# New instruction orders on four engines, the logits' copy on ScalarE and later pad writes in a one-core routing and expert kernel

## The reference, cut to what matters

```
x = x + L(layernorm(x))          # L: linear recurrent attention over T = 2048, B = 2, D = 256, 4 heads
    v = x @ W_write.T;  scores = (x_t . x_{s-1}) * decay;  reads = scores @ v + state @ x
    out + (alpha * reads) @ W_read.T
x = x + ffn(layernorm(x))        # ffn: 8 experts, each token through its best two
    logits = x @ gate_w.T; probs = softmax(logits); top 2
    h = gelu(x @ w1[e] + b1[e]); y = h @ w2[e] + b2[e]; sum over the two, times probs
```

## Time and profile before

| | us |
|---|---|
| median of 3 runs (lowest, highest) | 580.96 (578.54, 581.52) |
| the profiled execution | 579.32 |
| its span in the trace | 577.5 |
| PE / DVE / ACT / POOL busy | 532.7 / 457.7 / 332.8 / 243.4 |
| recurrent part and its overlap with the first tiles | 0 to about 205 |
| expert part | from 178, PE the bound after about 220 |

### The profile page before, as it was taken

The page is one execution under the profiler, slowest core; times in us unless marked ns, Lnnn a source line. Parts: engine busy times, 40 slices in busy tenths (PEclk is TensorE's granted clock), DMA queues, the critical chain, the costliest instruction groups (busy, mean ns, idle before and its releaser), DMA issues.

```text
span 577.5 us, 17639 instructions
## 1 busy us (share of the span) xinstructions
PE 532.7 (92%) x5246; PEld 417.3 (72%) x5246; DVE 457.7 (79%) x1408; ACT 332.8 (58%) x841; POOL 243.4 (42%) x275
## 2 busy tenths in 40 slices
PE   7788899897988977999999999999999999999991
PEld 7667777786777655777777777777777777777770
DVE  5889999998877789777787877787777887877761
ACT  5889888898735743454545444544454545444540
POOL 2425778887655632332233222333332333222333
PEclk8999999999899999999999999999999999999996
DMA  5667776867234442544443344444444443445432
GB/s 160 208 211 227 252 257 218 264 200 256 75 104 113 124 75 39 82 65 70 69 65 61 61 68 75 78 75 75 69 72 68 66 65 56 68 68 75 76 48 27
DMA packets 85097, 63.34 MB, mean 110 GB/s; under 512 B 54224, under 2 KB 77392, under 8 KB 85008
## 3 DMA queue, kind: packets, MB, share of 16 engines
q1 hardware_dynamic: 71328, 43.94, 30.0%
q0 software_dynamic: 13392, 18.27, 17.2%
q10 hardware_dynamic: 288, 0.00, 0.0%
HBM read 37.56 MB, written 24.62 MB: 108 GB/s over the span
## 4 chain that ended last, share of the span: by engine, by line
PE 60%; DVE 13%; POOL 9%; issue 8%; DMA 5%; ACT 2%; SPq 1%; another core or an unknown queue 0%; DVEq 0%; ACTq 0%; POOLq 0%
PE psum L1514 27%; PE psum L1529 18%; PE psum L1531 9%; POOL sent_rows L497 4%; DMA out<-arena,tile_in 2%; POOL tiny L487 2%; DVE arena L911 1%; DVE weights L775 1%; DMA arena<-sent_rows 1%; POOL tiny L484 1%; PE psum L1424 1%; PE psum L1334 1%; PE psum L1417 1%; PE psum L1345 1%; POOL out L528 1%
## 5 line engine op out<-in xcount | busy, mean ns | idle before, releaser
L1514 PE MATMUL psum<-arena,weights 128*128 128x256 f16 (+1 forms) x2208 | 278.7, 248 | 3.5 <-ACT arena L733 2.1
L1514 PEld LDWEIGHTS psum<-arena,weights 128*128 x2208 | 186.9, 98 | 81.9 <-issue 6.5
L733 ACT ACTIVATE arena<-psum,b_cur 128x256 f32<-128x256 f32 (+1 forms) x368 | 131.7, 424 | 157.7 <-PE psum L1514 119.9
L528 POOL DMA_INDIRECT out<-arena,tile_in x71 | 115.4, 1625 | 251.2 <-DVE arena L1157 147.0
L1529 PE MATMUL psum<-weights,arena 128*128 x568 | 214.7, 379 | 4.2 <-DVE arena L1144 3.9
L1531 PE MATMUL psum<-weights,arena 128*128 x568 | 154.8, 273 | 0.0
L1144 DVE TENSOR_TENSOR arena<-arena 128x512 f16<-128x512 f32 x142 | 99.6, 701 | 4.9
L497 POOL DMA_INDIRECT sent_rows<-arena,tiny x64 | 65.3, 1020 | 26.0 <-issue 18.3
L1142 DVE CAST arena<-arena 128x512 f16<-128x512 f32 x142 | 61.5, 433 | 7.3 <-ACT arena L733 6.6
L1529 PEld LDWEIGHTS psum<-weights,arena 128*128 128x128 f16 x568 | 55.5, 98 | 11.2 <-issue 5.3
L1531 PEld LDWEIGHTS psum<-weights,arena 128*128 128x128 f16 x568 | 55.6, 98 | 4.6 <-issue 0.2
(11 more groups left out here) (172 smaller groups left out, 643.4 us busy)
## 6 DMA issues: line engine op xcount, KB each, us to landing
weights<-in_experts SPq DMA_DIRECT2D x32, 512.0 KB, 4.5
arena<-sent_rows SPq DMA_DIRECT2D x100, 64.0 KB
arena<-in_b SPq DMA_DIRECT2D x46, 128.0 KB
arena<-in_x SPq DMA_DIRECT2D x16, 256.0 KB, 3.2
out<-arena SPq DMA_DIRECT2D x16, 256.0 KB
arena<-sent_rows SPq DMA_DIRECT2D x84, 32.0 KB
sent_rows<-pad SPq DMA_DIRECT2D x7, 265.0 KB
tile_in<-sent_rows SPq DMA_DIRECT2D x71, 4.5 KB, 3.0
```

Source lines behind the costliest of these rows:

```text
L528: pool.indirect_dma_start(out=out, out_offset=bass.IndirectOffsetOnAxis(ap=at_u, axis=0), in_=yout[:, u % 4], in_offset=None, compute_op=A ...
L733: last = a.activation(act[:, g % 2, m * n:(m + 1) * n], ps_h[:, g % 2, m * n:(m + 1) * n], ACT.Gelu_apprx_tanh, scale=1.0 / WSCALE, bias=b ...
L1514: last = pe.matmul(ps_h[:, f % 2, mm * n:(mm + 1) * n], w1_of(e_of[i], k, lo, per * (f - GROUP[i]) + mm), turned[:, i % 2, part, k, 0:n], ...
```

## The change

- `split_low`: from step 7 on (`n > ROUTED`) both remainders stand at the end of VectorE's step, behind `place`; before, the first stood behind `residual`. In steps 3 to 6 the first stays there.
- VectorE: `largest` goes ahead of `chunk_stats`, `carry` behind `residual`, `chunk_queries` behind `weigh_scores`; the copy of the logits (L869) leaves VectorE for ScalarE in steps 4 to 17.
- ScalarE: the first `split_high` goes ahead of `chunk_high`, the second ahead of `normed_transposed`, which goes ahead of `chunk_keys`; a third comes behind `chunk_normalise`; the logits' copy comes ahead of `normalise`.
- PE: `weigh` ahead of `values`, `states` behind `reads`.
- GpSimd: the code is put in functions; its order is as before.
- SP: the pads go from steps 6 to 12 to a place ahead of tile 4's waits, the write of zeros to the spare rows of `out` from step 6 to step 3.

```diff
+ROUTED = 6
@@ SP, step
-                if 6 <= n < 6 + E - 1:
-
-                    e = n - 6
-                    if e == 0:
-                        sp.wait_ge(setup_dve, 18)
-                        sp.wait_ge(setup_pool, 3)
...
-                    sp.dma_start(sent[e * CAP:e * CAP + TILE, :].rearrange("(p c) w -> p (c w)", c=2),
-                                 pad[:].rearrange("p c w -> p (c w)")).then_inc(pad_out, 16)
+                if n == 3:
+
+                    sp.wait_ge(setup_pool, 3)
...
@@ SP, tiles
                 if i == NE:
+                    for e in range(E - 1):
+                        sp.dma_start(sent[e * CAP:e * CAP + TILE, :].rearrange("(p c) w -> p (c w)", c=2),
+                                     pad[:].rearrange("p c w -> p (c w)")).then_inc(pad_out, 16)
                     sp.wait_ge(wide_done, 1)
@@ ScalarE
+            def logits(m):
+
+                reached(a, "logit_ps", m)
+                reached(a, "top_at_done", m - 1)
+                a.activation(logit, ps_logit, ACT.Copy).then_inc(S["logit_done"], 1)
...
                     last_column(n - 1)
+                for j in splits(n)[0:1]:
+                    split_high(j)
                 if active(n, 1):
                     chunk_high(n - 1)
-                for j in splits(n)[0:1]:
-                    split_high(j)
@@ VectorE
-                if active(n, 1):
-                    chunk_queries(n - 1)
                 if active(n, 3):
                     residual(n - 3)
-                for j in splits(n)[0:1]:
+                for j in splits(n)[0:1] if n <= ROUTED else ():
                     split_low(j)
+                if active(n, 3):
+                    carry(n - 3)
...
-                if active(n, 4):
-                    logits(n - 4)
...
+                for j in splits(n)[0:1] if n > ROUTED else ():
+                    split_low(j)
                 for j in splits(n)[1:]:
                     split_low(j)
@@ PE
                 if active(n, 2):
+                    weigh(n - 2)
+                if active(n, 2):
                     values(n - 2)
...
                 if active(n, 2):
                     reads(n - 2)
+                if 2 <= n <= NCH:
+                    states(n - 2)
```

More of the change, by code:

```diff
@@ new lines, in norm @@
+            def norm(m, moments, ve, rs, shift, got, mid, end, last, used, ago):
+                reached(pool, got, m)
+                reached(pool, used, m - ago - 1)
+                pool.tensor_scalar(ve, moments[:, :, 1], EPS, None, ALU.add)
+                pool.tensor_scalar(shift, moments[:, :, 0], -1.0, None, ALU.mult).then_inc(S[mid], 1)
+                reached(pool, mid, m)
+                pool.tensor_tensor(rs, ve, minus_half[:].to_broadcast([P, B]), ALU.pow).then_inc(S[end], 1)
+                reached(pool, end, m)
+                pool.tensor_tensor(shift, shift, rs, ALU.mult).then_inc(S[last], 1)
@@ new lines, in norm_chunk, with norm_residual, send @@
+            def norm_chunk(m):
+                s = m % 2
+                norm(m, moments1, ve1, rs1[s], shift1[s], "moments1_done", "ve1_done", "rs1_done", "shift1_done",
+                     "res_done", 1)
+            def norm_residual(m):
+                norm(m, moments2, ve2, rs2, shift2, "moments2_done", "ve2_done", "rs2_done", "shift2_done",
+                     "xm_done", 0)
+            def send(m, b):
+                if m == 0:
+                    pool.wait_ge(setup_dve, 18)
+                for name in ("token_done", "xm_done", "gates_done", "slot_i_done"):
+                    reached(pool, name, m)
+                for k in range(2):
+                    at_bk = slot_i[:, m % ROWS, 2 * b + k:2 * b + k + 1]
+                    pool.indirect_dma_start(
+                        out=sent, out_offset=bass.IndirectOffsetOnAxis(ap=at_bk, axis=0),
+                        in_=row[:, m % ROWS, b, :], in_offset=None).then_inc(row_out[m % ROWS], 16)
@@ L500, in step @@
+            def step(n):
+                if active(n, 0):
+                    norm_chunk(n)
+                if active(n, 3):
+                    norm_residual(n - 3)
+                if active(n, LAG):
+                    send(n - LAG, 0)
+                if active(n, LAG):
+                    send(n - LAG, 1)
                 if n == 2:
@@ L1449, in step @@
                 if active(n, 2):
+                    weigh(n - 2)
+                if active(n, 2):
                     values(n - 2)
-                if active(n, 2):
-                    weigh(n - 2)
                 if active(n, 5):
                     rank(n - 5)
-                if 2 <= n <= NCH:
-                    states(n - 2)
                 if active(n, 4):
```

57 lines of the change are left out of this document (18 added, 39 removed).

## The result

The changed kernel took 591.43 us (median of 10 runs, 583.2 to 622.05) where the kernel before took 580.72 (10 runs, 578.43 to 584.7) on the same chip. The ratio is 1.011, 95% interval 1.008 to 1.015: slower by about 1%. This ratio leaves out runs over 1.5% above a kernel's fastest, of which only the changed kernel had some, so it is the kinder of the two figures. The forecast was 576.5, in a range of 571 to 582. The profiled execution took 591.14, with a span of 589.4.

The account below looks back on a forecast made before the run. GpSimd, stretched by VectorE's remainders, was taken to bound the 10.28 us step. Steps 8 to 15 gain 4.6, step 7 loses 0.4, steps 3 to 6 lose 1.0: gain 3.2, giving 576.1 or 577.8; forecast 576.5, range 571 to 582.

Parts of the forecast that it names:

- What bounds the kernel: GpSimd sets the 10.28 us step; its short instructions, stretched beside VectorE's remainders, cost it 1.9 us a step.
- 9.7 per two-piece step: Steps 8 to 15, set by PE's round after the change, in place of 10.28: 4.6 us gained.
- Steps 3 to 7: Steps 3 to 6, a longer loop over three engines: 1.0 us lost; step 7, from 9.29 to 9.7: 0.4 lost.
- The detour on ScalarE: split_high ahead of chunk_high delays weigh: 2.8 us from turn_chunk's end, so PE stands about 0.5 each step.
- The disturbance in step 14: VectorE's unexplained 1.86 us at residual, then PE's lower clock: both left as they are, together plus or minus 1.5.
- A: Rival: ScalarE's added wait doesn't bind, steps take 9.35 us, gain 7.4, time 572; chance 0.18.
- B: Rival: the gain goes into another handover, GpSimd's factors reaching ScalarE late; steps 10.2 us, 580, no change; chance 0.22.
- C: Rival: both remainders hold the sends for their whole length; two-piece steps 10.8 us, 6.5 slower, 586; chance 0.10.
- The pads: SP's later pads delay tile 4's load by 7 us, hidden by a margin of about 3: zero cost.
- the tail: The work behind the recurrent part: it moves with that part, with no change of its own.

Follow-up runs that it names:

- before_third: The kernel before, unchanged, traced on a chip where it runs near 570 us: 569.87 us.
- b_late: The kernel before with only the weight remainders moved behind the sends' release from step 7 on: 570.40 us, ratio 1.001.
- b_stall: The kernel before with six stalls put in by hand (6.7 us in all) on ScalarE and VectorE: 580.74 us, ratio 1.001.
- after_third: The changed kernel, unaltered, on a chip where the kernel before takes 569.74 us: 570.49 us, ratio 1.001.
- before_again: The kernel before, unchanged, run beside the kernels with stalls put in by hand: 580.29 us.
- a_high_5: The changed kernel with chunk_high ahead of ScalarE's first split_high, on a chip where the kernel before takes 579.95 us: 610.23 us, ratio 1.051.
- a_high: The changed kernel with chunk_high ahead of ScalarE's first split_high: 566.23 us, ratio 0.994 to the kernel before.
- a_stall: The changed kernel with six stalls put in by hand (6.7 us in all) on ScalarE and VectorE: 600.93 us.

## Why the prediction was wrong

**What bounds the kernel: this step failed.** The prediction read the 0.22 us instructions that took 1.2 as the cause of the 10.28 us step, since one of them ended with VectorE's remainder, and took the 0.45 us wait of the residual as one that would go. It was the other way round. before_third has the stretch, at 0.67 and 1.13, in a step of 9.74, and b_late takes the stretch away and has 9.68: the stretch was worth 0.06 us a step, not a part of 1.9. On chip C b_stall has two stretched instructions (0.88 and 1.14) in a step of 9.62, and one (1.23) in a step of 10.25 with a stall on VectorE. The 0.54 between 9.74 and 10.28 is the residual's late release, which pushed the remainder, the statistics and GpSimd's round behind it. The sum also took 10.28 for all eight steps: four of them had about that length, steps 8, 12 and 15 took 9.61, 9.87 and 9.29, and step 14 took 13.32. The rows to see the late release in were there: in the earlier trace rows the reader starts 0.71 after its group's recorded end, where the prediction itself counted 0.05 for a handover.

**9.7 per two-piece step** held: 9.71 in the undisturbed step on chip A, 9.57 on B2 and D, and the same with the pads back on B and with plain sends on D, E and F. It was compared with the wrong base. On a quiet chip the base is 9.74, and the gain 0.17 a step: in seven of them before_third's lead at turn_chunk went from 85.43 - 83.50 = 1.93 to 152.43 - 151.71 = 0.72.

**Steps 3 to 7** were forecast to lose 1.4. Up to turn_chunk of step 9 after_third lost 1.7 against before_third (that lead of 1.93, less the 0.23 by which its first turn_chunk came later), of which 0.7 ahead of step 3, where the forecast had nothing; on chip A the steps 3 to 5 took 10.7 to 10.8, as forecast. Gain and loss nearly cancel, and the first tile load comes 1.1 later (163.70 to 162.59): the ratio of 1.001 to 1.002 on the quiet chips.

**The detour on ScalarE** was named, and mis-sized. The 0.5 us wait that it gives PE was there (0.65 in after_third), but moving chunk_high ahead gained only 0.10 in a two-piece step, 9.57 to 9.47. Most of the 4.5 us that this brought on D came from the steps with three pieces, on D from 10.7 to 9.8 in the first of them, for which the prediction gave the detour a loss of 0.25.

**The disturbance in step 14** was where the loss lay. The prediction saw the 1.86 us with no releaser and PE's clock behind it, and carried both over at plus or minus 1.5. The second follows the first (in before the granted clock is 0.50 from 145 to 147 us, behind PE's idle 1.54), and with the new order both come far more often: 9.8 us of "remote" waits ahead of the first token load in place of 1.9. In before and before_again the residual met them in steps 8 to 15, five times for about half a microsecond and three times for 1.9. In the new orders last_column meets them too, and it has everything behind it up to PE's weigh. A long one leaves PE idle for about 3 us. Then the clock falls: in a_high_5 values (L1422) takes 2.74 us where it took 1.49 undisturbed. Why the new orders have more of them is not shown. My reading is that in the old order ScalarE is still at reads_high when the first could meet it (last_column started 1.03 to 1.16 us after turn_chunk in steps 9 to 14 of before on A and 1.16 in those of before_third, where the new orders start it at 0.69), and stands ready beside the sends in the new ones. In a_high_5 the steps from 6 on stay at 11 to 16 us, and in each of those in which last_column came more than 3.5 us after turn_chunk the sends had begun 1.4 to 2.2 us ahead of turn_chunk, against 0.8 in after_third. But a_high on quiet chips has them up to 1.6 ahead in steps of 9.47, so this place alone makes no late release there, and that a late step brings about the next by this shift is a guess; no run tested it.

**The rivals.** A (572) and B (no change) were not it on chip A. B's size, though not its mechanism, is what the quiet chips show: 570.5 to 569.7. C, the sends held by the remainders, is refuted: they took 1.27 (1.08 before) and three times 0.96 or 0.97, and plain DMAs in their place left the step at 9.57. Its rule, that of the Trainium skill (SBUF — State Buffer, "Who interferes with whom"), agrees with the short instructions of before_third, and did not show in these sends. The Trainium skill has a condition in the same section that the prediction left out: a VectorE instruction with two inputs in SBUF, as a remainder is, contends with a GpSimd instruction that reads SBUF and not with one that only writes it. The case that did come was one which no rival had: late releases in many steps of the new order, at a reader with the whole step behind it.

**The pads, the tail.** Pads hidden, tile 4's load 7.4 later on D (forecast 7). The tail was equal: 409.8 and 409.3 on A, 405.7 and 405.8 on D.

The changed kernel gains on neither kind of chip. a_high gains 0.6% on the quiet ones and loses 5.1% on F.

## What to carry to other kernels

Before an idle time is priced, compare the start of the waiting instruction with the recorded end of what it waited for; where the distance is 0.7 us in place of 0.05, don't count on a new order to remove the wait. A wait that the profile puts down to nothing it can name is a price that any instruction at that place may have to pay: before moving instructions, look up what runs beside such waits and keep readers with a long chain behind them away from it. That this would have saved these 12 us is argued and not run. And a ratio from one chip can be that chip's: the same two kernels gave 1.011 on one and 1.001 or 1.002 on two others, where the intervals reach down to 1.000.

## What the runs showed of the hardware

- The same program took 580 us in three groups of runs and 570 in four, with no difference in the work. Where it took 580, instructions that read PSUM started late beside GpSimd's indirect sends, in the steps by 0.5 to 1.9 us in one order and by up to 3.7 in the others. Plain DMAs from the same queue, with as many packets and bytes in row q0 of the profile's page (13392, 18.27 MB), gave none on F.
- In a_high_5 all eight late starts of last_column with no releaser named came 0.8 to 1.0 us after the recorded end of the last send (94.04 after 92.19 + 0.96 = 93.15, in the rows above). In after and a_stall some came ahead of it. The Trainium skill (Perfetto Trace Analysis, "DMA Instruction — SWDGE (GPSIMD)") says that such a record ends when the descriptors are made, not when the data has moved. Whether making them, moving them, or the scattered rows holds TensorE's release back, no run here separates. Nor do the traces tell a late signal from a group that itself ended late, since the ends of matmuls in a profile are modelled.
- PE's granted clock fell to 0.50 some 0.6 us (a_high_5) and 1.3 us (after) after PE took up work again behind an idle time of 3.05 and 2.65 us, and stayed there for about three and nearly seven microseconds. In before it fell about 0.1 us after the work behind the idle 1.54 us began.
